# Moving the heads whose probabilities the DMA engines transpose two steps later in each group of an attention kernel

## The chip, the cores and the metric

The kernel runs on one core of a Trainium2 chip. The metric is the device time of one execution in microseconds (us). Three executions of the kernel before took 1040.63, 1045.36 and 1048.02 us, a median of 1045.36.

## The reference

The input x is 32 sequences of 32 tokens of width 512. Two layers are added to it. The first multiplies each sequence by a 32x32 weight that its subject number picks. The second, which holds nearly all of the work, is attention over a paged cache:

```
x = x + einsum('bct,bcd->bdt', x, weights[subjects])
q, k, v = x @ Wq.T, x @ Wk.T, x @ Wv.T      # 32 query heads, 8 key/value heads, D = 128
q, k = rope(rmsnorm(q)), rope(rmsnorm(k))
k_all = concat(k_cache[block_table], k)     # 512 cached keys + 32 new ones
v_all = concat(v_cache[block_table], v)
scores = q . k_all / sqrt(128), masked beyond the cached length
o = softmax(scores) . v_all
x = x + o.reshape(b, s, 4096) @ Wo.T
```

Each page holds 32 tokens, and every sequence names 16 pages in its own order. The cached length of a sequence only shifts the rope positions and the mask.

## The kernel before, in words

The program has two phases. The first (96 units of 128 tokens x 512 columns) projects q, k and v, normalises and rotates them, and writes queries, new keys, pages and values to DRAM as pairs of fp16 numbers, a high and a low part. The change does not touch it.

The second phase is one loop over STEPS steps. Head `i` here means one (sequence, key/value head) pair, 8 per sequence and 256 in all; its 128 rows are 4 query heads x 32 tokens. Each engine runs its own written-out loop over the steps, and semaphores tie them. At step `i` the engines work on different heads:

- PE (TensorE) transposes the probabilities of head `i` (`transpose_p`, L1460, four 128x128 fp32 transposes), computes the scores of head `i+3` (L1449 and L1453), weighs the values of head `i-2` (`weigh`, L1489, 12 matmuls), and every fourth step adds the new tokens' part (`weigh_new`, L1503).
- DVE (VectorE) takes the masked maximum of head `i+3` (L1154), the reciprocal of the row sums of head `i+2` (L1162), and the low part of the transposed probabilities (`t_lo`, L1174).
- ACT (ScalarE) takes the exponential of head `i+3` (L930) and the high part of the transposed probabilities (`t_hi`, L937).
- POOL (GpSimd) scales head `i+2` by the reciprocal (L865) and gathers the values of the next sequence into `vs` (L853).
- SP's queue loads everything else: the queries `qt` (L627), the edge keys (L629) and the 16 pages `kt` (L640) of the sequence after next, the new values `vn` (L649), and the results in and out.

Four sequences (32 steps) make a group, g0 to g7. When a group is done its output projection (`project_out`, L1411, 12 matmuls of 512 columns a step) is spread over steps 2 to 9 of the next group. It must wait for `ot_lo` (L1186), the low part of the last weighed heads. The projected halves are added to the residual on DVE (L1196) at steps 6 and 10.

For some heads, `by_dma(i)`, PE doesn't transpose. Instead ACT and DVE write the probabilities as two fp16 parts to a ring of three slots at the end of `wo` (`rows_hi`, L946, and `rows_lo`, L1169, at step `i-2`), and SP issues one DMA transpose into `pt` (`turn_rows`, L754). SP's loop issues it ahead of all other loads of loop number `i-2`, and waits there for `rows_lo` of that head and for the weighing of head `i-4`, which frees the buffer. DVE takes the reciprocal of such a head, and a second scalar (`split_by`, L1165), ahead of the masked maximum rather than behind it. PE waits for the landing just before it weighs the head.

The numbers that choose these heads are counted in steps of the group. In g1 the stretch begins at 8, not at DMA_FIRST, since conversions of Wo still run there.

Of the kernel before, what the change touches and what calls it, by code (L numbers as in the profile page):

```python
# [59 lines left out]
def build(nc, x, rows_in, table, l0_w, wq_t, wk_t, wv_t, wo_t, norms_in, kc_t, v_cache, wv,  # L60
# [371 lines left out]
        return n if rest == 0 and 0 <= n < NHB else None  # L432

    TN, TNE, OE = HPC - 1, HPC, HPC + 2
    DMA_FIRST, DMA_LAST, STAGED = 2, 11, 3

    def by_dma(i):

# [1206 lines left out]
```

## Time and profile before

| | |
|---|---|
| profiled execution | 1046.1 us |
| its span in the trace | 1044.3 us |
| PE busy | 982.7 us (94%) |
| DVE busy | 795.1 us (76%) |
| ACT busy | 717.4 us (69%) |
| POOL busy | 493.7 us (47%) |
| TensorE clock granted, mean | 0.993 of full speed |
| chain that ended last | PE 54%, DVE 16%, SP's queue 8%, DMA 7%, issue 6%, ACT 5%, POOL 2% |

The first table row is the device's own time of the execution that the trace records; the span is what the trace covers of it. Busy shares are averages over stages with different limits. In the chain each stretch of time is given to the engine or queue on which the end of the program waited just then.

### The profile page before, as it was taken

The page shows a single profiled execution, that of the slowest core. Times are in us where ns is not written, and L with a number is a line of the kernel's source. Part 1 is how long each engine was busy: PE and PEld are TensorE (multiplying, and loading weights), DVE is VectorE, ACT ScalarE, POOL GpSimd, SP SyncE. Part 2 cuts the span into 40 slices and gives each one's busy share as a digit, 9 for nine tenths or more (in the row PEclk, how much of TensorE's full clock was granted, in tenths as well). Part 3 has the DMA queues.
Part 4 walks back from the last instruction along what each step waited for, and adds up shares of the span by engine and source line. Part 5 has one row for each costly group of instructions (what it writes and reads, how often), then busy time and mean ns, then how long its engine had stood idle before and what let it go on. Part 6 is the DMA issues. An engine that isn't in the chain of part 4 may idle for free.

```text
span 1044.3 us, 24950 instructions
## 1 busy us (share of the span) xinstructions
PE 982.7 (94%) x8329; PEld 779.9 (75%) x8329; DVE 795.1 (76%) x1705; ACT 717.4 (69%) x1959; POOL 493.7 (47%) x642
## 2 busy tenths in 40 slices
PE   4889999999889999899999999998999999999998
PEld 2678888887678788769768857965976986895793
DVE  6779999999997788758847856865784885786680
ACT  4898999988765778747746746754774774675670
POOL 5445665566881266516415523622441641552340
PEclk9999999999999999999999999999999999999999
DMA  5789999989989899778998998999899999899740
GB/s 202 247 278 336 322 390 367 385 279 398 380 288 326 309 337 343 266 192 294 323 235 267 357 234 243 328 241 228 301 291 243 294 329 241 260 354 249 240 148 11
DMA packets 268016, 296.49 MB, mean 284 GB/s; under 512 B 94064, under 2 KB 225648, under 8 KB 265328
## 3 DMA queue, kind: packets, MB, share of 16 engines
q1 hardware_dynamic: 249200, 227.65, 71.3%
q0 software_dynamic: 18688, 67.25, 19.3%
q8 instruction: 67, 1.10, 0.4%
q14 instruction: 61, 0.50, 0.1%
HBM read 231.77 MB, written 46.27 MB: 266 GB/s over the span
## 4 chain that ended last, share of the span: by engine, by line
PE 54%; DVE 16%; SPq 8%; DMA 7%; issue 6%; ACT 5%; POOL 2%; ACTq 0%; DVEq 0%; POOLq 0%
PE ps_o L1411 16%; PE ps_proj L1411 15%; PE ps_o L1489 8%; SPq L640 5%; PE ps_s L1449 4%; PE ps_s L1453 4%; PE ps_t L1460 3%; DVE probs L1154 2%; DMA vs<-v_pages,v_row 2%; DMA kt<-k_pages_t 2%; PE ps_rt L1559 2%; DVE rot L1282 2%; DVE c_stage L1310 2%; PE ps_o L1503 1%; ACT probs L930 1%
## 5 line engine op out<-in xcount | busy, mean ns | idle before, releaser
L865 POOL TENSOR_SCALAR probs<-probs,recip 128x544 f32<-128x544 f32 (+1 forms) x256 | 157.5, 615 | 382.2 <-DVE recip L1162 377.7
L930 ACT ACTIVATE probs<-probs,neg_max 128x544 f32<-128x544 f32 x256 | 191.3, 747 | 155.5 <-DVE neg_max L1154 154.7
L1154 DVE CUSTOM_DVE_ANT_0 probs<-ps_s,mask,row_scale 128x544 f32<-128x544 f32 x256 | 200.1, 782 | 126.3 <-PE ps_s L1453 123.5
L1489 PE MATMUL ps_o<-pt,vs 128*128 128x128 f16 x3072 | 214.3, 220 | 8.2 <-DMA pt<-wo 3.8
L1489 PEld LDWEIGHTS ps_o<-pt,vs 128*128 128x128 f16 x3072 | 192.3, 98 | 19.0 <-issue 6.6
L821 POOL TENSOR_TENSOR roped<-rot 128x256 f32<-128x256 f32 x160 | 144.2, 922 | 82.2 <-DVE rot L1274 76.3
L1411 PE MATMUL ps_proj<-wt_hi,x0t_hi 128*128 128x512 f32 x384 | 159.7, 416 | 8.0 <-DVE x0t_lo L1112 7.0
L1411 PE MATMUL ps_o<-wo,ot_hi 128*128 128x512 f16 x512 | 153.7, 382 | 10.4 <-DVE ot_lo L1186 10.4
L1411 PE MATMUL ps_proj<-wt_hi,x0t_lo 128*128 128x512 f32 x384 | 151.7, 395 | 0.0
L1411 PE MATMUL ps_proj<-wt_lo,x0t_hi 128*128 128x512 f32 x384 | 150.8, 393 | 0.0
L853 POOL DMA_INDIRECT vs<-v_pages,v_row x128 | 131.4, 1026 | 22.3 <-issue 20.2
L1449 PE MATMUL ps_s<-kt,qt 128*128 128x256 f16 (+1 forms) x768 | 136.4, 287 | 1.9 <-DMA kt<-k_pages_t 1.7
L1174 DVE SCALAR_TENSOR_TENSOR pt<-ps_t,pt 128x512 f16<-128x512 f32 x192 | 130.7, 681 | 4.8 <-ACT pt L937 2.7
L1453 PE MATMUL ps_s<-kt,qt 128*128 128x288 f16 (+1 forms) x768 | 126.2, 273 | 6.7 <-DVE neg_max L1154 6.5
L1460 PE MATMUL ps_t<-fixed,probs 128*128 128x128 f32 x768 | 117.6, 276 | 2.3 <-POOL probs L865 1.1
L937 ACT ACTIVATE pt<-ps_t 128x512 f16<-128x512 f32 x192 | 111.2, 579 | 5.3 <-PE ps_t L1460 5.3
L998 ACT ACTIVATE squares<-ps_proj 128x128 bf16<-128x128 f32 x320 | 85.1, 296 | 21.7 <-PE ps_proj L1411 21.6
L1411 PE MATMUL ps_o<-wo,ot_lo 128*128 128x512 f16 x256 | 97.6, 381 | 0.0
L1453 PEld LDWEIGHTS ps_s<-kt,qt 128*128 128x128 f16 x768 | 73.4, 98 | 27.5 <-DVE neg_max L1154 12.9
L1411 PEld LDWEIGHTS ps_o<-wo,ot_hi 128*128 128x128 f16 x512 | 47.7, 98 | 59.5 <-DVE ot_lo L1186 9.8
L1411 PEld LDWEIGHTS ps_proj<-wt_hi,x0t_hi 128*128 128x128 f32 x384 | 72.9, 190 | 25.2 <-DVE x0t_lo L1112 11.8
L1449 PEld LDWEIGHTS ps_s<-kt,qt 128*128 128x128 f16 x768 | 74.2, 98 | 22.0 <-DMA kt<-k_pages_t 3.2
(146 smaller groups left out, 1599.0 us busy)
## 6 DMA issues: line engine op xcount, KB each, us to landing
kt<-k_pages_t SPq DMA_DIRECT2D x512, 128.0 KB
c_nat<-in_L_cond_k_cache SPq DMA_DIRECT2D x32, 512.0 KB, 5.8
q_t<-stage SPq DMA_DIRECT2D x64, 256.0 KB, 7.3
c_nat<-in_L_cond_v_cache SPq DMA_DIRECT2D x32, 512.0 KB, 7.2
qt<-q_t SPq DMA_DIRECT2D x32, 512.0 KB, 6.2
w_nat<-in_L_cond_Wq SPq DMA_DIRECT2D x8, 1024.0 KB, 8.9
k_pages_t<-c_stage SPq DMA_DIRECT2D x16, 512.0 KB, 5.8
c_nat<-in_L_cond_Wo SPq DMA_DIRECT2D x16, 512.0 KB, 7.7
```

The lines of the kernel that those rows point to most:

```text
L821: last = pool.tensor_tensor(dst, a, b, ALU.add)
L853: pool.indirect_dma_start(vs[b % 2][:, c].rearrange("p j s d -> p (j s d)"), None, v_pages, bass.IndirectOffsetOnAxis(ap=v_row[:, b * NCH ...
L865: pool.tensor_scalar(part, part, col(recip, i), 1.0, ALU.mult, ALU.mult).then_inc(p_norm, 1)
L930: act.activation(pr, pr, ACT.Exp, bias=col(neg_max, i), scale=-1.0, accum_out=col(row_sum, i)).then_inc(a_exp, 1)
L937: act.activation(pt_part(i, 0), ps_t[tjob_no["t", i] % NTB][:], ACT.Copy, scale=P_SCALE).then_inc(a_thi, 1)
L1154: dve.tensor_tensor_reduce(out=probs_of(i), in0=ps_s[:, score_cols(i):score_cols(i) + KEYS], in1=mask[(i // HK) % 2][:, mask_at(i):mask_at ...
L1174: dve.scalar_tensor_tensor(pt_part(i, 1), ps_t[tjob_no["t", i] % NTB][:], P_SCALE, pt_part(i, 0), ALU.mult, ALU.subtract).then_inc(v_tlo, 1)
L1411: ins = pe.matmul(ps, a, b, start=first and n == 0, stop=last and n == len(pairs) - 1)
L1449: pe.matmul(own[0], q[:, a], k[:, b, own[1]:own[2]], start=n2 == 0, stop=n2 == 2)
L1453: ins = pe.matmul(shared[0], q[:, a], k[:, b, shared[1]:shared[2]], start=n2 == 0, stop=n2 == 2)
L1460: ins = pe.transpose(ps_t[tjob_no["t", i] % NTB][:, c * P:(c + 1) * P], probs_of(i)[:, SEQ * (i % 2) + c * P:SEQ * (i % 2) + (c + 1) * P], ...
L1489: ins = pe.matmul(ps_o[n % 2][:, jl * P:(jl + 1) * P], v[:, part, :], pt[i % NPT][:, NCH * half + c, :], start=jl == 0 and c == 0 and k == ...
```

## The change

The heads that the DMA engines transpose are steps 4 to 13 of a group in place of 2 to 11. Nothing else in the text is changed; every engine's loop asks `by_dma`, so all of them move.

```diff
     TN, TNE, OE = HPC - 1, HPC, HPC + 2
-    DMA_FIRST, DMA_LAST, STAGED = 2, 11, 3
+    DMA_FIRST, DMA_LAST, STAGED = 4, 13, 3
 
     def by_dma(i):
 
         g, r = divmod(i, GSTEPS)
         return 0 < i < NP2 and g >= 1 and (DMA_FIRST if g > 1 else 8) <= r <= DMA_LAST
```

In g2 to g7 there are ten such heads before and after. In g1, which begins at 8, there are six in place of four.

The first place is SP's queue in loops 9 to 13 of group g5: `pt` rows are the transposes, `vn` the new values, `qt` the queries with which the loads of the fourth sequence begin. Before:

```order
L754 DMA_TRANSPOSE pt3<-wo 128x8x128
L649 DMA vn0<-v_new 32x4x256 x2
L649 DMA vn0<-v_new 32x4x128 x2
L627 DMA qt1<-q_t 128x2048
L629 DMA kt1<-k_new_t 128x2x256
```

And with the change:

```order
L754 DMA_TRANSPOSE pt3<-wo 128x8x128
L754 DMA_TRANSPOSE pt0<-wo 128x8x128
L649 DMA vn0<-v_new 32x4x256 x2
L649 DMA vn0<-v_new 32x4x128 x2
L754 DMA_TRANSPOSE pt1<-wo 128x8x128
L627 DMA qt1<-q_t 128x2048
L629 DMA kt1<-k_new_t 128x2x256
```

The transposes of heads 12 (into pt0) and 13 (into pt1) now stand ahead of the queries, and the loads of the new values stand between them.

The second place is DVE at steps 10 to 12 of the same group. Before:

```order
L1196 SCALAR_TENSOR_TENSOR result1<-ps_o0,y_unscale,result1 128x512
L1154 ISA probs,neg_max<-ps_s,mask1,row_scale 128x544
L1154 ISA neg_max 128x1
L1162 RECIPROCAL recip<-row_sum 128x1
L1186 SCALAR_TENSOR_TENSOR ot_lo<-ps_o1,ot_hi 128x16x32
L1154 ISA probs,neg_max<-ps_s,mask1,row_scale 128x544
```

And with the change:

```order
L1196 SCALAR_TENSOR_TENSOR result1<-ps_o0,y_unscale,result1 128x512
L1162 RECIPROCAL recip<-row_sum 128x1
L1165 TENSOR_SCALAR split_by<-recip 128x1
L1154 ISA probs,neg_max<-ps_s,mask1,row_scale 128x544
L1154 ISA neg_max 128x1
L1186 SCALAR_TENSOR_TENSOR ot_lo<-ps_o1,ot_hi 128x16x32
L1169 SCALAR_TENSOR_TENSOR wo<-probs,split_by,wo 128x512
L1162 RECIPROCAL recip<-row_sum 128x1
L1165 TENSOR_SCALAR split_by<-recip 128x1
L1154 ISA probs,neg_max<-ps_s,mask1,row_scale 128x544
```

The low parts of heads 12 and 13 (L1169) now come here, and the reciprocals of these heads stand ahead of the maximum.

The third place is DVE at the start of the group, steps 0 and 1, up to the low part of the previous group's last heads. Before:

```order
L1169 SCALAR_TENSOR_TENSOR wo<-probs,split_by,wo 128x512
L1174 SCALAR_TENSOR_TENSOR pt0<-ps_t1,pt0 128x512
L1162 RECIPROCAL recip<-row_sum 128x1
L1165 TENSOR_SCALAR split_by<-recip 128x1
L1154 ISA probs,neg_max<-ps_s,mask0,row_scale 128x544
L1154 ISA neg_max 128x1
L1169 SCALAR_TENSOR_TENSOR wo<-probs,split_by,wo 128x512
L1174 SCALAR_TENSOR_TENSOR pt1<-ps_t2,pt1 128x512
L1186 SCALAR_TENSOR_TENSOR ot_lo<-ps_o1,ot_hi 128x16x32
```

And with the change:

```order
L1174 SCALAR_TENSOR_TENSOR pt0<-ps_t2,pt0 128x512
L1154 ISA probs,neg_max<-ps_s,mask0,row_scale 128x544
L1154 ISA neg_max 128x1
L1162 RECIPROCAL recip<-row_sum 128x1
L1174 SCALAR_TENSOR_TENSOR pt1<-ps_t0,pt1 128x512
L1186 SCALAR_TENSOR_TENSOR ot_lo<-ps_o1,ot_hi 128x16x32
```

The two low parts for the DMA transposes (L1169) are gone from these steps; `t_lo` of heads 2 and 3 has come to steps 2 and 3.

## Rows read from the trace of the kernel before

**Rows 1.** The page: shares of the chain that ended last, by line.

```profile
PE ps_o L1411 16%; PE ps_proj L1411 15%; PE ps_o L1489 8%; SPq L640 5%; PE ps_s L1449 4%; PE ps_s L1453 4%; PE ps_t L1460 3%; DVE probs L1154 2%; DMA vs<-v_pages,v_row 2%; DMA kt<-k_pages_t 2%; PE ps_rt L1559 2%; DVE rot L1282 2%; DVE c_stage L1310 2%; PE ps_o L1503 1%; ACT probs L930 1%
```

**Rows 2.** Busy time by stretch: one group; then two pieces of g5.

```profile
core 0: us, PE busy (x) PEld busy (x) DVE busy (x) ACT busy (x) POOL busy (x), PEclk, DMA share, GB/s
517.00:600.00 83.00, 80.32 (x840) 64.10 (x840) 59.62 (x157) 53.26 (x117) 34.93 (x48) 1.00 0.98 281
...
812.00:816.00 4.00, 4.00 (x55) 3.75 (x53) 3.00 (x9) 2.91 (x7) 3.42 (x5) 1.00 0.62 174
820.00:824.00 4.00, 4.00 (x54) 3.76 (x52) 3.58 (x10) 3.09 (x8) 1.43 (x2) 1.00 1.04 389
```

**Rows 3.** Timeline of PE, start of g3: start us, us, instruction, [idle before].

```profile
600.38 0.46 PE L1453 MATMUL ps_s<-kt,qt 128*128 128x224 f16 x3 [0.65 <-DVE neg_max L1154]
...
602.76 1.03 PE L1411 MATMUL ps_o<-wo,ot_hi 128*128 128x512 f16 x2 [1.26 <-DVE ot_lo L1186]
```

**Rows 4.** Timeline of DVE, same place.

```profile
600.32 0.75 DVE L1169 SCALAR_TENSOR_TENSOR wo<-probs,split_by,wo 128x512 f16<-128x512 f32 x1
...
602.01 0.69 DVE L1186 SCALAR_TENSOR_TENSOR ot_lo<-ps_o,ot_hi 128x512 f16<-128x512 f32 x1 [0.34 <-ACT ot_hi L963]
```

**Rows 5.** Timeline of ACT, same place.

```profile
601.40 0.58 ACT L963 ACTIVATE ot_hi<-ps_o 128x512 f16<-128x512 f32 x1
```

**Rows 6.** Timeline of PE, start of g1, where no head is transposed by DMA yet.

```profile
434.21 0.59 PE L1411 MATMUL ps_o<-wo,ot_hi 128*128 128x512 f16 x2 [1.87 <-DVE ot_lo L1186]
```

**Rows 7.** Timeline of PE, steps 10 to 14 of g5.

```profile
810.19 0.83 PE L1489 MATMUL ps_o<-pt,vs 128*128 128x128 f16 x12 [0.35 <-DVE result L1196]
...
812.44 0.60 PE L1460 MATMUL ps_t<-fixed,probs 128*128 128x128 f32 x4
812.88 0.57 PE L1449 MATMUL ps_s<-kt,qt 128*128 128x320 f16 x3
...
817.63 0.83 PE L1489 MATMUL ps_o<-pt,vs 128*128 128x128 f16 x12
```

**Rows 8.** Timeline of DVE, steps 9 and 10 of g5.

```profile
809.18 0.75 DVE L1196 SCALAR_TENSOR_TENSOR result<-ps_o,y_unscale,result 128x512 f32<-128x512 f32 x1 [2.25 <-PE ps_o L1411]
...
810.66 0.67 DVE L1186 SCALAR_TENSOR_TENSOR ot_lo<-ps_o,ot_hi 128x512 f16<-128x512 f32 x1
```

**Rows 9.** Timeline of SP's queue, g5: time an issue takes on the queue.

```profile
808.01 1.25 SPq L754 DMA_TRANSPOSE pt<-wo  x1
809.30 2.50 SPq L649 DMA_DIRECT2D vn<-v_new  x4
813.77 0.35 SPq L627 DMA_DIRECT2D qt<-q_t  x1
...
815.25 9.81 SPq L640 DMA_DIRECT2D kt<-k_pages_t  x16
...
829.56 0.32 SPq L627 DMA_DIRECT2D qt<-q_t  x1
```

**Rows 10.** The chain that ended last, in order of time, g5.

```profile
824.73 6.07 DMA kt<-k_pages_t
830.84 0.50 PE ps_s L1449 x3
```

**Rows 11.** Timeline of PE: waits for pages at the end of g2.

```profile
589.44 0.50 PE L1449 MATMUL ps_s<-kt,qt 128*128 128x256 f16 x3 [0.29 <-DMA kt<-k_pages_t]
```

**Rows 12.** DMA transposes (line 754), issue to landing, all of them.

```profile
DMA to landing us min/median/max: 2.8/4.0/11.8
```

**Rows 13.** The same, those of g2 issued between 521 and 526 us.

```profile
DMA to landing us min/median/max: 5.2/5.8/6.4
```

**Rows 14.** Timeline of PE, g4, head 11.

```profile
729.94 1.46 PE L1489 MATMUL ps_o<-pt,vs 128*128 128x128 f16 x12 [3.78 <-DMA pt<-wo]
```

**Rows 15.** Busy time by stretch, behind the waits in g3 and g4.

```profile
602.00:606.00 4.00, 3.23 (x8) 1.19 (x9) 2.75 (x8) 2.28 (x4) 2.25 (x4) 0.60 1.19 254
726.00:734.00 8.00, 4.22 (x31) 3.62 (x30) 1.80 (x5) 2.58 (x6) 2.96 (x4) 0.69 1.07 323
```

## The prediction

> **What bounds the kernel now.** I read the busy shares first, then the chain that ended last, then the timelines of PE and of SP's queue in one group. In a group PE is busy 80.3 of 83.0 us at the full clock, and the DMA engines are busy too, 0.98 of the time [rows 2]. So the second phase is a PE program with little room beside it. The chain says who else is in the path: the page loads of SP's queue (L640) hold 5% of the span and the landing of `kt` 2% [rows 1].
>
> Three things cost PE time around the stretch. At the start of a group PE waits 0.65 us for a masked maximum and 1.26 us for `ot_lo` [rows 3]; the same pair stands in all six groups g2 to g7, with 0.86 for the second in g5. At step 10 it waits 0.35 us for the residual [rows 7]. Later in the group it waits for pages: 0.29 us in one place [rows 11], and in g5 the chain runs from SP's queue through the landing of the last page, 6.07 us, to the scores [rows 10]. That wait looks small, but it marks deliveries that arrive just when they are needed. In g5 the queries are issued at 813.77, the 16 pages take the queue 9.81 us, and PE starts on them at 830.84, 17.1 us after the queries [rows 9, 10]. The queue then goes on to the next sequence without a rest, at 829.56 [rows 9].
>
> **The change, part by part.** The sum is made against the profiled execution, 1046.1 us, of which the span is 1044.3. It is 0.7 above the median of the runs.
>
> *PE transposes.* Four of them take 0.44 us of PE (812.44 to 812.88) [rows 7]. Heads 2 and 3 come back to PE and heads 12 and 13 leave it; in g1 two leave and none comes.
>
> *Start of a group (g2 to g7).* Steps 0 and 1 lose two `rows_lo` of 0.75 us on DVE [rows 4] and two `rows_hi` on ACT, which do the same 128x512 elements; I take 0.7 us each. `ot_hi` starts at 601.40 behind ACT's queue [rows 5]; without 1.4 us of work ahead it can start at 600.0 and end at 600.6, and `ot_lo`, 0.69 us [rows 4], ends at 601.3. PE without its waits would be ready at 602.76 - 1.91 + 0.44 = 601.3 as well. So the projection starts 1.4 us earlier with head 2's transposes included, and head 3's take 0.44 back: 1.0 us gained per group. Rows_lo and `t_lo` of heads 2 to 5 now share steps 2 and 3, but those steps have projection on PE, 16% of the span over 64 steps or 2.6 us each [rows 1], which hides them. The bounds: at best 1.91 - 0.88 = 1.0 gained; at worst the wait stays as long as at the start of g1, 1.87 us [rows 6], where no head is split, and 1.87 + 0.88 - 1.91 = 0.8 is lost. I take the gain, because in g1 the conversions of Wo stood in ACT's and DVE's way, and they are over by g2. Six groups: -5.8 us.
>
> *Steps 10 to 13.* PE saves 0.88 us. DVE gets two `rows_lo` and four scalars, in steps that have no projection left to cover them. After the residual ends at 809.93 [rows 8] come 0.3 us of scalars, 0.78 of maximum, 0.67 of `ot_lo` and 0.75 of `rows_lo`: head 12's rows are ready at 812.4, head 13's at about 814.3. The maxima of heads 14 and 15 come 0.8 us late and PE waits for them. The bounds are 0.9 gained and 0.6 lost; near the middle PE weighs head 12 at 817.6 as now [rows 7]. I count nothing, because of the next term: whoever reaches the next pages early waits there.
>
> *SP's queue, which decides.* Now the transpose of head 11 is issued at 808.01, the new values at 809.30, and the queue then waits for the scores of head 15, and issues the queries at 813.77 [rows 9]. After the change the queue stands still until head 12's rows are ready. Then come, in order, head 12's transpose 812.4 to 813.7 (1.25 us), the new values to 816.2 (2.50), head 13's transpose to 817.4 (1.25), and only then the queries, at 817.45: 3.7 us later. With the pages behind them, the last page is issued 3.7 us later. It lands between two bounds. The late one is 3.7 us later, with the same 6.07 us from issue to landing [rows 10]. The early one has the DMA engines emptied in the meantime: 3.7 - (6.07 - 2.8) = 0.4 later, with the fastest landing of any transpose here [rows 12] as the shortest time. I take 3.1, near the late bound: the engines don't empty, since two transposes of 256 KB are added just there, and between 812 and 816 only 0.38 of four us was free [rows 2], while from 820 on the share is 1.04. The next sequence's loads follow without a pause [rows 9], so that the lateness stays and is paid once in a group, not twice.
>
> The waits for pages [rows 10, 11] say that PE has no slack to set against it; I take that for g1, g2, g3, g5, g6 and g7. In g4 it has some: PE lost 3.78 us to a late head 11 [rows 14] and ran at half clock behind it [rows 15], so its pages were there long before. There I count zero. Six groups: +18.6 us.
>
> The sum is 1046.1 - 5.8 + 18.6 = 1058.9 us, and 0.7 less for the median: 1058 us.
>
> Work that costs nothing: POOL scales 32 columns in place of 544 for heads 12 and 13, and the reverse for 2 and 3, and nobody waits for POOL at either place. The new values are needed a whole sequence later. The ring of three slots is as full as before.
>
> **The rivals.** *The queue is hidden* (13%). The lateness of 3.7 us on SP's queue doesn't reach PE, because the time of a delivery is the DMA engines' and not the queue's. Then only the start of the group changes: 1046.1 - 5.8 - 0.7 = 1040 us, below the kernel before. It decides where less than 1.0 us of the 3.7 arrives at PE in each group. For it speaks the DMA share of 1.04 [rows 2]; against it the 9.81 us that 16 issues take and the chain through L640 [rows 1, 9, 10].
>
> The Trainium skill, in "DMA: Bandwidth & Descriptors", section "Issuing engines are not separate DMA queues", says that the sequencer's time to start a DMA is usually small relative to the DMA itself. By that rule this rival is what would happen, at 1040 us. The trace doesn't agree: here the issues fill 9.81 of the 17.1 us.
>
> *The engines catch up* (14%). The last page lands 0.4 to 1.5 us late, near the early bound. With 0.9 a group this gives 1046.1 - 5.8 + 6 x 0.9 - 0.7 = 1045 us, no change.
>
> *The clock falls too* (12%). The forecast's wait is a gap of some 3 us in PE's work in each group. Behind the 3.78 us wait in g4 the granted clock averaged 0.69 over 8 us, and in g3 it was 0.60 behind waits of 1.91 us in all [rows 14, 15]; the other groups with the same 1.91 us kept the full clock. Half speed for 3.4 to 7 us costs 1.7 to 3.5 us. In most of seven groups that adds 10 to 18 us: 1068 to 1076, say 1071. Head 13 landing late makes this likelier: issued at 816.2 with the 5.2 to 6.4 us that transposes take beside gathers [rows 13], it lands after 821, and PE wants it at about 819.8.
>
> **The numbers.** The forecast has 58%, with a range of its own of 1052 to 1067 from 2.1 to 3.7 us a group and a fall of the clock or two; 3% stay for anything else. The range of all is 1041 to 1070: it leaves out half of the first rival and some of the last. A change below 1%, 10.5 us, can't be told from none here. Faster than 1034.9 is then 3%, since not even the first rival gets there; within 1% are both milder rivals and the lower tail of the forecast, 39%; slower than 1055.8 is 58%.
>
> **What would show it.** Right, if in SP's queue the queries of the fourth sequence follow head 13's transpose without a gap, some 3.7 us after PE's scores of head 15; if PE then waits 2 to 3.7 us for `kt` at step 21 (the scores of head 24), once a group, g1 included; and if the waits of 0.65 and 1.26 us at the start of g2 to g7 shrink to under 0.5 in all. Wrong, if the pages land in 14 us or less from the queries, if the queries go out before 815.5 in g5's terms, or if PE spends its waits on `pt` of heads 12 and 13 with no wait for `kt` behind.

## The result, and the profile after

The kernel now takes 1094.4 us, median of four runs (1080.7 to 1098.7), against 1046.0 for the kernel before on the same chip (1040.6 to 1048.0). The ratio of the two means is 1.0427, with a 95% interval of 1.0322 to 1.0533; it leaves out the longest run, 1098.7 us, as a slow one. The forecast was 1058 us with a range that ended at 1070. The direction was right; the loss is four times the 12 us forecast.

The profiled execution took 1080.7 us, the shortest of the four, and is 34.6 us above the profiled execution before. The other three ran at a lower mean clock, 0.972 to 0.975 against 0.984. From the page, the chain of waits by line, and the group of weighing matmuls (busy us, mean ns of one | idle before them and its cause):

```profile
PE ps_o L1411 15%; PE ps_proj L1411 12%; PE ps_o L1489 8%; DMA pt<-wo 4%; PE ps_s L1449 4%; PE ps_s L1453 4%; SPq L640 4%; PE ps_t L1460 4%; DMA kt<-k_pages_t 2%; DVE probs L1154 2%; SPq L649 2%; DMA w_nat<-in_L_cond_Wq 2%; DVE rot L1282 2%; DVE c_stage L1310 2%; PE ps_rt L1559 2%
L1489 PE MATMUL ps_o<-pt,vs 128*128 128x128 f16 x3072 | 216.9, 221 | 39.6 <-DMA pt<-wo 33.6
```

Against [rows 1] a new member stands in the chain, the landing of transposed heads (`DMA pt<-wo`) with 4%. PE waits 33.6 us for them, where it had waited 3.8 us before, all of that in g4 [rows 14]. The list of waits from 440 us on (us in total, times, longest) begins with these:

```profile
PE ps_o L1489 <- DMA pt<-wo: 33.6, 12, 6.9
PE ps_s L1449 <- DMA kt<-k_pages_t: 4.1, 4, 2.0
PE ps_s L1453 <- DVE neg_max L1154: 3.2, 7, 0.8
PE ps_o L1489 <- DVE result L1196: 2.5, 7, 0.4
PE ps_o L1411 <- DVE ot_lo L1186: 2.1, 5, 1.4
PE ps_o L1489 <- DVE ot_lo L1186: 1.5, 1, 1.5
```

The last of these is misnamed: `ot_lo` had ended long before, and that matmul too waited for a transpose (below). So 35.1 us in 13 waits go to `pt`: 14.0 us in six waits for head 12 and 21.1 us in seven for head 13. Pages, the forecast's term, cost 4.1 us. These four waits stand at step 29 of their groups; at step 21, where the forecast put them, the change has none.

Start of g3 on PE, which answers [rows 3]; and the group before it by stretch, which answers [rows 2]:

```profile
611.40 0.60 PE L1411 MATMUL ps_o<-wo,ot_hi 128*128 128x512 f16 x2 [0.18 <-DVE ot_lo L1186]
```

```profile
core 0: us, PE busy (x) PEld busy (x) DVE busy (x) ACT busy (x) POOL busy (x), PEclk, DMA share, GB/s
523.00:611.40 88.40, 82.28 (x840) 65.14 (x840) 59.46 (x158) 53.55 (x116) 35.06 (x48) 0.98 0.94 268
```

The two waits at the start, 1.91 us, have become 0.18. The group takes 88.4 us in place of 83.0, and the DMA engines move less in a microsecond than before (268 GB/s against 281).

The place is steps 12 and 13. In g5, PE (start, us, [idle before]):

```profile
831.47 0.46 PE L1453 MATMUL ps_s<-kt,qt 128*128 128x224 f16 x3 [0.40 <-DVE neg_max L1154]
...
835.21 0.45 PE L1453 MATMUL ps_s<-kt,qt 128*128 128x224 f16 x3
837.21 0.83 PE L1489 MATMUL ps_o<-pt,vs 128*128 128x128 f16 x12 [1.54 <-DVE ot_lo L1186]
...
841.55 0.84 PE L1489 MATMUL ps_o<-pt,vs 128*128 128x128 f16 x12 [2.16 <-DMA pt<-wo]
```

SP's queue at the same time, which answers [rows 9]:

```profile
822.16 1.25 SPq L754 DMA_TRANSPOSE pt<-wo  x1
824.13 1.89 SPq L640 DMA_DIRECT2D kt<-k_pages_t  x4
826.12 5.76 SPq L754 DMA_TRANSPOSE pt<-wo  x2
831.94 2.50 SPq L649 DMA_DIRECT2D vn<-v_new  x4
834.54 1.50 SPq L754 DMA_TRANSPOSE pt<-wo  x1
836.08 0.58 SPq L627 DMA_DIRECT2D qt<-q_t  x1
836.71 0.56 SPq L629 DMA_DIRECT2D kt<-k_new_t  x1
837.85 9.55 SPq L640 DMA_DIRECT2D kt<-k_pages_t  x16
```

And POOL's queue, which the prediction had left out:

```profile
828.60 1.02 POOL L853 DMA_INDIRECT vs<-v_pages,v_row  x1
...
830.92 1.01 POOL L853 DMA_INDIRECT vs<-v_pages,v_row  x1 [0.16 <-issue]
...
833.86 1.02 POOL L853 DMA_INDIRECT vs<-v_pages,v_row  x1 [0.16 <-issue]
...
835.81 1.01 POOL L853 DMA_INDIRECT vs<-v_pages,v_row  x1 [0.17 <-issue]
```

The row of two transposes at 826.12 holds head 11's and then head 12's, which the chain shows issued at 830.33. Head 12 is weighed at 837.21, 6.9 us after its issue; the last of the 16 signals that tell of its landing stands in the trace 6.7 us after it. Head 13, issued at 834.54, is weighed at 841.55. In the view of line 754 issue to landing of that one is 7.0 us, and of the one at 822.16 (head 10's), which has no gather beside it, 2.9 us. This view times only transposes into buffers of `pt` for which the trace has every landing signal, half of all here and none of the heads 12. Over those that it times:

```profile
DMA to landing us min/median/max: 2.7/3.7/12.5
```

The longest is head 13's of g3; over the seven groups head 13 takes 7.0 to 12.5 us.

The four gathers of the values for the group's third sequence are issued in POOL's loops 10 to 13, in every group, before and after the change. Before, the stretch of transposes ended just ahead of them: in g5 head 11's was issued at 808.01 [rows 9] and the first gather at 811.71.

Gathers as such are no new company, though. Heads 4 to 7 go out beside the second sequence's four gathers, in both kernels. With the change, in g5, their transposes are issued from 796.40 to 808.18 and the gathers from 795.18 to 805.39. One of these gathers, and the landing of heads 5 and 6, the two that the view times there:

```profile
801.47 1.02 POOL L853 DMA_INDIRECT vs<-v_pages,v_row  x1 [0.16 <-issue]
...
DMA to landing us min/median/max: 3.0/4.0/5.0
```

In the six groups these two heads take 2.9 to 5.8 us, and PE never waits for them.

**The account.** By the profiled executions: waits for `pt` +31.3 us (35.1 against 3.8), for pages +2.4, for `ot_lo` and the maximum -7.2 (5.3 against 12.5). The mean granted clock fell from 0.993 to 0.984. With its two levels, full and half speed, that is 2 x 0.007 x 1044 = 15 us at half speed before and 2 x 0.016 x 1079 = 35 us now; 20 us more at half speed cost about 10. The sum is 36.5 us, and 34.6 were measured. In the other three runs, of which there is no trace, the mean clock says that 55 to 61 us were at half speed; by the same estimate that costs 10 to 13 us more and leads to 1091 to 1094, if their waits were the same. The rows around the ends of two of the long waits show the fall (PEclk is the third number from the end):

```profile
core 0: us, PE busy (x) PEld busy (x) DVE busy (x) ACT busy (x) POOL busy (x), PEclk, DMA share, GB/s
569.00:577.00 8.00, 7.18 (x71) 6.46 (x72) 3.43 (x9) 3.47 (x8) 1.44 (x2) 0.79 1.08 355
...
664.00:672.00 8.00, 8.00 (x88) 7.41 (x89) 4.13 (x10) 4.36 (x9) 1.44 (x2) 0.83 1.01 325
```

### The profile page after: what moved, and what is told of

Same layout as the page of the kernel before. It is cut to its first block, busy times and chain, and to the rows that moved or that the text cites. A ratio compares the mean times of both kernels' runs of the same rounds, so it can differ in the third digit from the quotient of the medians.

```text
span 1078.9 us, 24945 instructions
## 1 busy us (share of the span) xinstructions
PE 992.1 (92%) x8321; PEld 783.5 (73%) x8321; DVE 793.3 (74%) x1707; ACT 720.6 (67%) x1959; POOL 494.0 (46%) x642
## 3 DMA queue, kind: packets, MB, share of 16 engines
q0 software_dynamic: 18688, 67.25, 19.3%
## 4 chain that ended last, share of the span: by engine, by line
PE 52%; DVE 15%; DMA 11%; SPq 9%; issue 6%; ACT 5%; POOL 2%; ACTq 0%; DVEq 0%; POOLq 0%
PE ps_o L1411 15%; PE ps_proj L1411 12%; PE ps_o L1489 8%; DMA pt<-wo 4%; PE ps_s L1449 4%; PE ps_s L1453 4%; SPq L640 4%; PE ps_t L1460 4%; DMA kt<-k_pages_t 2%; DVE probs L1154 2%; SPq L649 2%; DMA w_nat<-in_L_cond_Wq 2%; DVE rot L1282 2%; DVE c_stage L1310 2%; PE ps_rt L1559 2%
## 5 line engine op out<-in xcount | busy, mean ns | idle before, releaser
L1489 PE MATMUL ps_o<-pt,vs 128*128 128x128 f16 x3072 | 216.9, 221 | 39.6 <-DMA pt<-wo 33.6
L1460 PEld LDWEIGHTS ps_t<-fixed,probs 128*128 128x128 f32 x760 | 82.9, 144 | 6.6 <-issue 3.6
```

What stands on the lines that cost most here:

```text
L1460: ins = pe.transpose(ps_t[tjob_no["t", i] % NTB][:, c * P:(c + 1) * P], probs_of(i)[:, SEQ * (i % 2) + c * P:SEQ * (i % 2) + (c + 1) * P], ...
L1489: ins = pe.matmul(ps_o[n % 2][:, jl * P:(jl + 1) * P], v[:, part, :], pt[i % NPT][:, NCH * half + c, :], start=jl == 0 and c == 0 and k == ...
```

## The experiments

All times are medians beside runs of the kernel before on the same chip, whose median lay between 1043.3 and 1046.4 us. "Waits" are PE's in the profiled execution, from 440 us to the end, by the name that the list of waits gives them: the change has 1.5 us and e9 3.1 us more for `pt` under another name. Twelve kernels were run; a summary first.

| kernel | median us | ratio, 95% | PE waits: pt / pages / gathered values |
|---|---|---|---|
| before (2 to 11) | 1046 | | 3.8 / 1.7 / 0.5 |
| the change (4 to 13) | 1094.4 | 1.0427 (1.032 to 1.053) | 33.6 / 4.1 / 0.5 |
| e1: 4 to 11 | 1036.2 | 0.990 (0.984 to 0.996) | 0 / 1.6 / 2.5 |
| e2: 2 to 13 | 1099.5 | 1.050 (1.044 to 1.056) | 46.5 / 2.4 / 0.4 |
| e3: 4 to 12 | 1059.0 | 1.011 (1.004 to 1.018) | 0.8 / 19.2 / 2.7 |
| e4: change, no gathers of the third sequence | 1068.8 | 1.020 (1.014 to 1.026) | 1.5 / 30.5 / 1.5 |
| e5: change, new values loaded a step earlier | 1073.6 | 1.026 (1.019 to 1.034) | 29.9 / 0 / 1.6 |
| e6: e3 and new values earlier | 1036.2 | 0.992 (0.989 to 0.995) | 0.2 / 2.7 / 2.6 |
| e7: before, no gathers of the third sequence | 1042.4 | 0.999 (0.996 to 1.002) | 0 / 2.7 / 0.3 |
| e8: e4 and e5 together | 1042.4 | 0.999 (0.996 to 1.002) | 0 / 13.0 / 1.6 |
| e9: e5, head 13 held back | 1093.2 | 1.046 (1.040 to 1.052) | 31.8 / 7.9 / 1.5 |
| e10: e5, without head 12 | 1062.0 | 1.017 (1.012 to 1.022) | 19.3 / 3.1 / 1.7 |
| e11: e5, all four gathers 4 loops later | 1107.9 | 1.061 (1.057 to 1.065) | 0 / 0 / 55.4 |
| e12: e5, two of the gathers later | 1097.2 | 1.053 (1.049 to 1.057) | 28.1 / 0 / 19.6 |

**e1, the start alone.** The stretch begins two heads later but still ends at 11.

```diff
-    DMA_FIRST, DMA_LAST, STAGED = 4, 13, 3
+    DMA_FIRST, DMA_LAST, STAGED = 4, 11, 3
```

> The new first head with the old last one: heads 4 to 11 of a group, eight in place of ten (four in g1, as before). If the whole loss of the change stands at the end of the stretch, this kernel has only the gain at the start: the PE waits for the masked maximum and for ot_lo at the start of g2 to g7 shrink from 1.91 to under 0.3 us, PE gets 0.88 us of transposes back in each of the six groups, 12 to 13 us of SP's queue and two transposes' traffic go away. Expected 1036 to 1043 us, that is 3 to 9 us below the kernel before, and no wait for pt over 1 us. If the late start costs something too, as the worse bound of my prediction had it, it is 1046 to 1051.

Measured 1036.2 us (1034.2 to 1038.0), 1% below the kernel before. PE waits no more for `pt`, and the start of g3 has

```profile
601.80 0.60 PE L1411 MATMUL ps_o<-wo,ot_hi 128*128 128x512 f16 x2 [0.19 <-DVE ot_lo L1186]
```

So the first term of the sum was right in sign and place, and the other half of the change costs about 58 us (1094.4 - 1036.2). The gain is somewhat over the 5.8 us forecast; the profile has two reasons for it, the 3.8 us wait of g4, which is gone too, and a mean clock of 0.998.

**e2, the end alone.**

```diff
-    DMA_FIRST, DMA_LAST, STAGED = 4, 13, 3
+    DMA_FIRST, DMA_LAST, STAGED = 2, 13, 3
```

> The old first head with the new last one: heads 2 to 13, twelve in a group (six in g1). If the loss belongs to heads 12 and 13 alone it is all here, and the gain at the start is not: the changed kernel's time plus 4 to 8 us, 1085 to 1105 us, with PE waits for pt of some 34 us or more in the profile, all at steps 14 and 15. If instead the loss needs the late start (as when the transposes of heads 4 to 11 ran later and pushed the last two), it comes out below 1070.

Measured 1099.5 us (1090.3 to 1108.9). PE waits 46.5 us for `pt` in the profiled execution, which was the longest of the six; 1.4 of them are for another head. The loss belongs to heads 12 and 13 whatever the start does.

**e3, one head less.**

```diff
-    DMA_FIRST, DMA_LAST, STAGED = 4, 13, 3
+    DMA_FIRST, DMA_LAST, STAGED = 4, 12, 3
```

> Heads 4 to 12: of the two late heads only the first. Theory of the gathers (transposes issued beside the four value gathers of POOL's loops 10 to 13 land in 7 us and more, whatever the queue holds): head 12 still waits at step 14, about 1.5 to 2.5 us a group, and the time is 1050 to 1062. Theory of the queue (the new values' four loads stand between heads 12 and 13 and make head 13 late; head 12 is only late because of head 13's traffic): no wait over 0.5 us and 1038 to 1046.

Measured 1059.0 us (1053.3 to 1063.8). Here the wait that I had forecast stands alone:

```profile
PE ps_s L1449 <- DMA kt<-k_pages_t: 19.2, 7, 3.6
PE ps_o L1489 <- DMA vs<-v_pages,v_row: 2.7, 5, 0.9
PE ps_o L1411 <- DVE ot_lo L1186: 1.8, 3, 1.4
PE ps_o L1489 <- DMA pt<-wo: 0.8, 1, 0.8
```

Seven waits for pages, 2.7 us each, all at step 21, g4 included. The page term exists; in the full change another wait comes ahead of it and hides it. Neither theory of the expectation fits: head 12 alone lands in time beside the gathers (0.8 us of waits in all), and the time is still 13 us above the kernel before.

**e4, the gathers taken away.** The kernel of the change without the four value gathers of the third sequence of each group; that sequence is weighed with what the buffer held, so its own part of the output is left out.

```diff
                 for c in chunks:
+                    if b % GB == 2:
+                        continue
                     pool.indirect_dma_start(
...
-                    pe.wait_ge(d_vs[b % 2], 16 * NCH * (b // 2 + 1))
+                    pe.wait_ge(d_vs[b % 2], 16 * NCH * (b // 2 + 1 if b % 2 else b // 4 + 1))
```

> The changed kernel without the value gathers of the third sequence of each group (the ones that POOL issues in loops 10 to 13, beside the transposes of heads 12 and 13); this sequence is weighed with the values of the one two before it. Theory of the gathers: with them gone the two transposes land in 3 to 4 us, the PE waits for pt fall from 34 us to under 5, and the time falls by 30 to 45 us, to about 1040 to 1055. Theory of the queue: the order on SP's queue is the same, head 13 is still issued 2.5 us late and the queries 3.7 us late, so that at least half of the waits stay and the time is above 1065.

Measured 1068.8 us (1066.4 to 1069.3). The waits, with lines two further down:

```profile
PE ps_s L1451 <- DMA kt<-k_pages_t: 30.5, 7, 5.4
PE ps_o L1413 <- DVE ot_lo L1188: 2.1, 5, 1.4
PE ps_o L1491 <- DMA pt<-wo: 1.5, 2, 1.2
```

Without these gathers heads 12 and 13 land in time: by their landing signals in the trace they take 2.7 to 4.6 us. What had been behind now shows, seven waits for pages of 4.4 us each, at step 21. The waits for `pt` went as the theory of the gathers said, but the time is above the 1065 us that the expectation gave to the theory of the queue: both are at work.

**e7, the control.** The same gathers left out of the kernel before.

> Control: the kernel before without the value gathers of the third sequence of each group (it is weighed with the values of the one two before it). It tells what this traffic costs by itself. I expect 1038 to 1045 us: PE waits little for it, and pages landed just in time before, so that at most the waits for pages (1.7 us) and the one wait for pt (3.8 us) go.

Measured 1042.4 us (1038.4 to 1049.5), the ratio 0.9986 with an interval across 1. So less traffic as such is worth little, 2.5 us by the medians; nearly all of the 25.6 us between the change and e4 belongs to the meeting of gathers and transposes.

**e5, e8 and e6, the queue.** The four loads of new values stand on SP's queue between head 12's transpose and head 13's. Here those of the third sequence are issued one step earlier, ahead of head 12's.

```diff
-                if r == 2 and 1 <= b < B - 1:
+                if r == (1 if b % GB == 1 else 2) and 1 <= b < B - 1:
```

> The changed kernel with the new values of the third sequence loaded one loop earlier on SP's queue, in loop 9 behind head 11's transpose, as they stood in time before the change; heads 12 and 13 then follow each other and the queries come 1.9 us late in place of 3.7 to 4.4. Gathers theory (the transposes are slow because their 256-byte packets interleave with the gathers' 4096-byte ones): head 13 is issued some 2.5 us earlier but still lands in 6 us or more, PE waits for pt stay at 15 us or more, and the time is 1060 to 1080. Queue theory (the late issue of head 13 is what hurts): waits for pt below 8 us, time 1045 to 1058.

Measured 1073.6 us (1063.3 to 1078.3). The waits for pages are gone (4.1 to 0), and those for `pt` are 29.9 us, now all before head 12, since both transposes go out 2 us apart and land together. With the gathers left out as well (e8, the same part left out as in e4):

> The changed kernel without the value gathers of the third sequence of each group, and with the new values loaded one loop earlier. Without the gathers alone it took 1068.8 us, with 30.5 us of waits for kt, one of 3.1 to 5.4 us in each group. If the place of SP's loads sets them, the queries leave 2.5 us earlier in each of seven groups: waits for kt 10 to 16 us, time 1048 to 1056. If the engines' work sets them, nothing changes: 1065 or more.

Measured 1042.4 us (1038.6 to 1050.1). The four corners with heads 4 to 13 are then 1094.4, 1073.6 (values earlier), 1068.8 (no gathers) and 1042.4 (both). The last is level with e7, the kernel before with the same work left out, so that the loss against the kernel before hangs on these two. It is not level with e1, since 13.0 us of waits for pages are left, now all at step 29. The same edit on e3:

> Heads 4 to 12 with the new values loaded one loop earlier. The kernel with heads 4 to 12 took 1059 us and waited 19.2 us for kt and 0.8 for pt. If those 19.2 us come from the place of the new values on SP's queue (head 12's transpose 1.25 us and four loads of 2.50 us stand between its rows and the queries), they go: waits for kt under 4 us, 1034 to 1042 us, level with heads 4 to 11. If they come from the DMA engines' work (one more transpose in the busy stretch), the order doesn't matter and the time stays at 1053 or above.

Measured 1036.2 us (1032.3 to 1037.2), down from 1059.0, with 2.7 us of waits for pages in place of 19.2. This version beats both kernels of the case; it is level with e1.

**e9, is it the pair?** A rival to the gathers alone was that two transposes in flight slow each other. SP holds head 13's until head 12's has landed.

```diff
+                if i % GSTEPS == DMA_LAST:
+                    landed(sp, i - 1)
                 sp.dma_start_transpose(
```

> The changed kernel with the new values one loop earlier (1073.6 us, PE waits for pt 29.9 us, all for head 12, which lands 8.4 to 10.4 us after its issue, within 1 us of head 13), and with SP's queue holding head 13's transpose back until head 12's has landed. Theory of the pair (two transposes in flight beside the gathers slow each other, since head 12 alone landed without a wait): head 12 lands in under 6 us and its waits go; head 13 is issued some 5 us after head 12, lands late by 2 to 4 us and takes the wait over, in part; the queries are late too. 1055 to 1068 us. Theory of the gathers alone (each transpose there takes 8 us and more): head 12 still waits 3 to 5 us a group, head 13 as much again, 1090 us or more.

Measured 1093.2 us (1087.4 to 1097.0), slower than e5. Head 12's transpose, with no other behind it, was issued at 830.38 in g5, and both PE and SP's queue, which waits for the same landing, had to wait until 840.7:

```profile
840.77 1.44 PE L1491 MATMUL ps_o<-pt,vs 128*128 128x128 f16 x12 [5.05 <-DMA pt<-wo]
```

POOL's gathers were issued at 828.65, 830.98, 833.91 and 835.87. The pair is not what makes it late. Head 13's transpose, issued at 840.71 behind the last gather, was weighed at 844.64 without a wait. Over the seven groups head 12 cost 26.6 us of waits and head 13 8.3, less than the "as much again" of the expectation.

**e10, head 13 alone.**

```diff
-        return 0 < i < NP2 and g >= 1 and (DMA_FIRST if g > 1 else 8) <= r <= DMA_LAST
+        return 0 < i < NP2 and g >= 1 and (DMA_FIRST if g > 1 else 8) <= r <= DMA_LAST and r != 12
```

> Heads 4 to 11 and 13, with the new values one loop earlier: the later of the two late heads alone, nine in a group. Theory of the pair: a single transpose beside the gathers lands within 6 us, PE doesn't wait for pt (under 3 us in all), and the queries are late by head 13's rows and transpose only: 1038 to 1048 us. Theory of the gathers alone or of lateness within the gathers (head 13 stands later among them than head 12 does): waits for pt of 10 us or more, 1055 us or more.

Measured 1062.0 us (1058.1 to 1065.3); 19.3 us of waits for `pt` in seven. One transpose, issued at 818.07 among gathers at 816.27, 818.34, 820.28 and 822.23, is weighed at 825.84. In e6 one transpose at 801.16, among gathers at 799.43, 802.89, 804.84 and 806.79, is weighed at 806.61. So a single transpose beside gathers is weighed 7.8 us after its issue in one kernel and 5.4 in the other.

**e11, all gathers moved away.** With the values loaded earlier, POOL issues the third sequence's gathers in its loops 14 to 17. All traffic is there; only the meeting is not.

```diff
-                if rest in V_SLOTS and 2 <= b + 1 < B:
-                    load_v(b + 1, V_SLOTS.index(rest))
+                slot = rest - 4 if (b + 1) % GB == 2 else rest
+                if slot in V_SLOTS and 2 <= b + 1 < B:
+                    load_v(b + 1, V_SLOTS.index(slot))
```

> The changed kernel with the new values one loop earlier, and with the four gathers of the third sequence issued in POOL's loops 14 to 17 in place of 10 to 13, all work done. If the gathers beside them make the transposes of heads 12 and 13 late, the waits for pt (29.9 us) fall under 4 us, although all of the traffic is still there. The gathered values are then wanted at step 18, one step after the last gather's issue, and PE waits for vs 2 to 3 us a group: 1050 to 1065 us. If the transposes are late for another cause, the waits for pt stay over 15 us and the time is above 1080.

Measured 1107.9 us (1106.7 to 1110.8), and the waits are

```profile
PE ps_o L1490 <- DMA vs<-v_pages,v_row: 55.4, 11, 8.7
PE ps_o L1412 <- DVE ot_lo L1187: 3.5, 4, 1.7
```

No wait for `pt` is left; by their landing signals heads 12 and 13 take 2.7 to 4.0 us, where e5's took 7.3 to 10.4. The longest landing in the view of line 754, 6.7 us, belongs to head 5 of g6, beside the second sequence's gathers. The cause is shown without leaving work out. It is no cure: in each group PE now waits 7 to 9 us for the values, where 2 to 3 were expected and where it waited 3 to 5 us for the transposes in e5.

**e12, two of four.** By then I held that the number of gathers beside the transposes sets their lateness. The last two go into loops 14 and 15.

```diff
-                if rest in V_SLOTS and 2 <= b + 1 < B:
-                    load_v(b + 1, V_SLOTS.index(rest))
+                slots = (0, 1, 4, 5) if (b + 1) % GB == 2 else V_SLOTS
+                if rest in slots and 2 <= b + 1 < B:
+                    load_v(b + 1, slots.index(rest))
```

> Heads 4 to 13 and the earlier load of the new values (as in e5, 1073.6 us), and of the third sequence's four value gathers the last two are issued by POOL in its loops 14 and 15 instead of 12 and 13; the first two stay in loops 10 and 11. Theory now: what makes the transposes of heads 12 and 13 late is how many gathers' packets are in the DMA engines between their issue and their landing. With two of four taken away from there PE's waits for pt should fall from 29.9 us to 5 to 15 (longest under 4), and the waits for vs grow, since the last gather is some 4 us later, about half of the 55 us that four moved gathers gave: 10 to 30 us. The sum is then about where e5 is or above, 1060 to 1095 us. Rival: any gather beside a transpose is enough; then the waits for pt stay at 25 to 35 us and the time is over 1090. Second rival: only the last two gathers matter, because the first two are done before head 13's rows are ready; waits for pt under 2 us.

Measured 1097.2 us (1092.8 to 1103.8), with 28.1 us of waits for `pt` in seven: my theory of the number fell, and of the expectation's cases the first rival fits, that one gather beside the two transposes is enough here. In g5 the first gather had moved 116 of its 128 packets when the first packets of head 12's transpose ran, at 850.5, and nearly only the second, issued at 849.21, ran beside the two transposes (issued from 848.75 on, 3.95 us for both). Head 12 was weighed at 857.87, after a wait of 3.93 us. The stretches below have DMA share and GB/s as their last two numbers. They are a transpose without a gather, a gather without a transpose, and the two kinds together (with the next queries behind them):

```profile
core 0: us, PE busy (x) PEld busy (x) DVE busy (x) ACT busy (x) POOL busy (x), PEclk, DMA share, GB/s
846.20:847.40 1.20, 0.87 (x14) 0.90 (x15) 1.17 (x6) 0.76 (x2) 0.81 (x2) 1.00 0.95 215
849.50:850.50 1.00, 0.74 (x11) 0.74 (x12) 1.00 (x4) 0.86 (x4) 0.72 (x1) 1.00 0.95 373
850.50:858.00 7.50, 3.57 (x47) 2.93 (x44) 4.00 (x12) 3.84 (x10) 3.17 (x4) 1.00 1.21 166
```

Together they move 166 GB/s with the engines busy all the time, less than either alone. In 7.5 us that is 1.25 MB. Two transposes of 256 KB at 215 GB/s would take 2.4 us, and the remaining 0.72 MB at 373 GB/s 1.9 us: 4.3 us in place of 7.5, an estimate from one stretch of each kind.

The Trainium skill, in "DMA: Bandwidth & Descriptors", section "Queues, rings and completion order", says that each DMA engine goes round the queues for which it has work, packet by packet. By that rule a transpose is held up by a gather's packets, as it is here. It would leave the sum of the two times as it is, and the 4.3 us against 7.5 show that this is not the whole cost here.

## Why the prediction was wrong

**Start of a group: right.** Forecast -1.0 us a group. The waits fell from 1.91 to 0.18 us and the projection gained 1.73, less 0.88 of two heads' PE transposes: 0.85. e1 shows the gain alone.

**PE transposes and the order on SP's queue: right.** The queries follow head 13's transpose without a gap, at 836.08. The scores that release them (those at 813.29 in the kernel before) end now at 831.47 + 0.46 = 831.93: 4.15 us earlier than the queries, where 3.7 was forecast.

**The page term: right as a mechanism, too small, and hidden.** Forecast 3.1 us in six groups, with g4 at zero. Where nothing hides it, it is 4.4 us in seven (e4) and 2.7 us in seven for one head less (e3), always at step 21 as forecast, and g4 pays it too (3.1 and 2.4 us). The loads that cause it, moved one step, bring 1059.0 to 1036.2. In the change itself PE waits for pages 4.1 us in all and never at step 21, so that this sign of being right didn't come.

**Steps 10 to 13, "I count nothing": this is the step that failed.** The prediction wrote that "whoever reaches the next pages early waits there", and so let the page wait absorb any lateness of heads 12 and 13. It is the other way round. The lateness was the larger of the two, it came first, and it absorbed the pages' wait: 35.1 us of waits for `pt`, 5.0 a group, in place of nothing. The wait for the maximum that this part also looked at is 0.4 us in six groups (the row at 831.47) and 0.8 in g3.

Behind it lies a price taken from the wrong row. For head 13's landing the text used "the 5.2 to 6.4 us that transposes take beside gathers" [rows 13] and put it after 821 against a need at 819.8. From 816.2 that is 1.6 to 2.8 us late by the prediction's own numbers, and even this was used only to make a rival likelier and stood in no sum. Head 13 in g5 took 7.0 us, and over the groups 7.0 to 12.5. The row isn't false for heads early in the group (with the change heads 5 and 6 take 2.9 to 5.8 us there), but it doesn't carry over to steps 12 and 13. The 11.8 us of [rows 12] and the 3.78 us of [rows 14] were the warning: both are of g4, the first of head 6, which went out beside gathers too, and the one group in which the old stretch ran into trouble already cost 3.8 us. And head 12 wasn't priced at all. Its new place is among POOL's loops 10 to 13. The passage on work that costs nothing asked whether POOL is late there, not what POOL issues there.

**The rivals.** "The queue is hidden" came out false by e3 and e6. The Trainium skill's rule on it, in "DMA: Bandwidth & Descriptors", section "Issuing engines are not separate DMA queues", that the time to start a DMA is usually small relative to the DMA, is not borne out here either: four small loads hold SP's queue for 2.50 us, and moving them from ahead of the queries is worth 22.9 us (e3 against e6). "The clock falls too" (12%) named the right consequence, and named head 13 as what would make it likelier; but the waits behind which the clock fell were those for `pt` and not for pages, and it priced the whole at 1071. Its clock term of 10 to 18 us is close to the estimates of 10 us (profiled execution) and 20 to 23 us (the others). The prediction's last sentence listed waits on `pt` of heads 12 and 13, with none for `kt` behind, as what would prove it wrong. That is what came, but for 4.1 us at step 29; it had given that case no chance and no time.

**What is open.** It is shown that the third sequence's gathers cause the waits for heads 12 and 13 (e4, e11, with e7 as control), that head 12 is late without a second transpose in flight (e9), and that two transposes with little more than one gather beside them are late enough (e12). Not settled is why a single transpose beside gathers takes 5.4 us in e6 (and lands nearly in time in e3) but takes 7.8 in e10 and 10.4 in e9, why heads 5 and 6 beside the second sequence's gathers take no more than 5.8, and what within the DMA engines slows both kinds when they run together. The runs give no rule for it. The gap between POOL's first two gathers was 3.5 us in e6, 2.1 in e10 and 2.3 in e9; beside head 4 in g5 of the change (6.3 us by its landing signals) it was 2.4 us as well, but the third gather came 3.9 us later, against 1.9 in e10 and 2.9 in e9. That the spacing decides was not tested by a run of its own.

## What to carry to other kernels

Before a transfer with a deadline is moved to another step, list what every queue issues around that step, the queues of the engines that "nobody waits for" among them, and take its landing time from rows with that company, at their worst and not at their median (here 11.8 us and not 5.2 to 6.4). When two late deliveries follow each other, price each as if the other weren't there: the longer and earlier one hides the other, and taking it away shows the second (e4). A stretch that holds two independent edits, here its start and its end, is to be tried one end at a time: the start alone gains 1%, the end alone loses 5%.

## What the runs showed of the hardware

- DMA transposes issued by SP and gathers issued by POOL slow each other: 166 GB/s together at a DMA share of 1.21, against 215 and 373 GB/s apart at 0.95 (e12). A transpose of 256 KB lands 2.7 to 4.0 us after its issue without gathers (heads 12 and 13, e8) and 7.0 to 12.5 us beside the third sequence's gathers (head 13, the change). Beside gathers it can also take 2.9 to 5.8 us (heads 5 and 6, the change). The Trainium skill, in "Advanced Engine Details and Errata", section "X-Bar Transpose (TRN2)", says that transpose DMAs are as fast as regular ones; the rows above show 215 against the 373 GB/s of a gather in this kernel.
- With 13 waits of PE for `pt` of 0.5 to 7.0 us in seven groups, the mean granted clock was 0.984, and 0.972 to 0.975 in the runs without a trace, against 0.993 before. In the 8 us around or behind the ends of the waits of 3.64 and 6.95 us it was 0.79 and 0.83, part of that time at half speed and the rest at full.
